# Slot experts: the last two experts' first matrices are loaded ahead of their second ones, and the tokens' keys and values are projected in pieces, with changes to routing and to the order of two engines

## The reference: what is computed

```
    o = q + _mha(q, x, x, d_...)                      # 16 slots of each batch
    h = layernorm(o)
    u = silu(h @ e_W1[e] + e_b1); g = silu(h @ e_Wg[e] + e_bg)
    o = o + (u * g) @ e_W2[e] + e_b2                  # slot e by expert e
    out = _mha(x, o, o, c_...)                        # keys o @ c_Wk, values o @ c_Wv
```

## Time and profile before

| what | before |
|---|---|
| median of 3 runs | 933.26 us (930.7 to 937.52) |
| profiled execution, own time | 932.76 us |
| its span in the trace | 931.0 us |
| PE busy | 827.4 us, 89% |
| DVE, ACT busy | 578.5 us, 511.6 us |
| routing block, until PE starts the next | 61.38 us |
| routed experts' last output product starts | 318.3 us |
| slot experts, first product to last result | 778.7 to 869.7 us |
| last block | from 871.0 us |

### The profile page before, as it was taken

The page is one execution under the profiler, slowest core; times in us unless marked ns, Lnnn a source line. Parts: engine busy times, 40 slices in busy tenths (PEclk is TensorE's granted clock), DMA queues, the critical chain, the costliest instruction groups (busy, mean ns, idle before and its releaser), DMA issues. The chain is left out here.

```text
span 931.0 us, 20572 instructions
## 1 busy us (share of the span) xinstructions
PE 827.4 (89%) x8132; PEld 705.6 (76%) x8132; DVE 578.5 (62%) x929; ACT 511.6 (55%) x935; POOL 196.0 (21%) x243
## 2 busy tenths in 40 slices
PE   5489999999999878999999989999998965976797
PEld 5389898999899756777788879999997952432354
DVE  3747778777787357887778855454435744321296
ACT  3138788788787245676767873433324432422364
POOL 0022434345343212234212222000000000000052
PEclk9599999999999989999999999999998986988799
DMA  7048676777684213432031112000008743998321
GB/s 294 1 174 324 209 286 214 271 260 253 214 301 131 62 52 81 87 74 42 19 137 48 41 52 92 1 1 1 1 1 341 295 197 118 425 427 348 125 82 69
DMA packets 70423, 143.21 MB, mean 154 GB/s; under 512 B 42504, under 2 KB 48136, under 8 KB 62904
## 3 DMA queue, kind: packets, MB, share of 16 engines
q1 hardware_dynamic: 64224, 127.25, 38.3%
q0 software_dynamic: 4496, 12.53, 3.9%
q10 hardware_dynamic: 1608, 2.12, 0.6%
HBM read 128.38 MB, written 13.50 MB: 152 GB/s over the span
## 5 line engine op out<-in xcount | busy, mean ns | idle before, releaser
L541 POOL DMA_INDIRECT results_of_experts<-k_w_ff,moew_place_of x39 | 56.1, 1439 | 147.4 <-DMA results_of_experts<-k_w_ff,moew_place_of 74.5
L87 PE MATMUL moe_pH<-moe_hh,moew_wh 128*128 128x256 f32 x256 | 72.5, 283 | 3.9 <-DVE moe_hl L758 3.9
L88 PE MATMUL moe_pH<-moe_hh,moew_wl 128*128 128x256 f32 x256 | 71.7, 280 | 0.0
L89 PE MATMUL moe_pH<-moe_hl,moew_wh 128*128 128x256 f32 x256 | 71.7, 280 | 0.0
L758 DVE TENSOR_TENSOR moe_hl<-k_w_ff,moe_hh 128x512 fp32r<-128x512 f32 x64 | 44.3, 691 | 33.9 <-ACT moe_hh L697 30.5
L688 ACT ACTIVATE k_w_ff<-moe_pH,moe_b 128x256 f32<-128x256 f32 x128 | 53.3, 467 | 17.8 <-PE moe_pH L89 13.4
L738 DVE TENSOR_TENSOR moew_wl<-k_x,moew_wh 128x1024 fp32r<-128x1024 f32 x45 | 53.4, 1218 | 1.3 <-ACT moew_wh L660 1.3
L738 DVE TENSOR_TENSOR moew_wl<-moew_raw,moew_wh 128x1024 fp32r<-128x1024 f32 x44 | 52.1, 1220 | 2.4 <-ACT moew_wh L660 2.2
L1710 DVE TENSOR_TENSOR k_w_ff<-attn_pS,k_w_ff 128x512 f32<-128x512 f32 x32 | 22.1, 691 | 50.3 <-PE attn_pS L89 34.6
L87 PEld LDWEIGHTS moe_pH<-moe_hh,moew_wh 128*128 128x128 f32 x256 | 48.2, 188 | 5.3 <-DVE moe_hl L758 5.3
L1484 ACT ACTIVATE attn_wh<-k_w_ff 128x512 fp32r<-128x512 f32 x32 | 20.2, 632 | 52.5 <-DVE k_w_ff L1710 52.5
(11 more groups left out here) (422 smaller groups left out, 2756.2 us busy)
## 6 DMA issues: line engine op xcount, KB each, us to landing
ring<-in_w_slot SPq DMA_DIRECT2D x10, 2048.0 KB
k_x<-in_w SPq DMA_DIRECT2D x24, 512.0 KB
k_x<-in_w SPq DMA_DIRECT2D x12, 1024.0 KB
moew_raw<-in_w SPq DMA_DIRECT2D x22, 512.0 KB
moew_raw<-in_w SPq DMA_DIRECT2D x11, 1024.0 KB
ring<-in_w_slot SPq DMA_DIRECT2D x9, 1024.0 KB, 16.8
k_w_ff<-in_w_slot SPq DMA_DIRECT2D x4, 2048.0 KB
attn_gat<-results_of_experts SPq DMA_DIRECT2D x16, 256.0 KB, 3.5
```

What stands on the lines that cost most here:

```text
L87: nc.tensor.matmul(out, ah, bh, start=start, stop=False)
L88: nc.tensor.matmul(out, al, bh, start=False, stop=False)
L89: return nc.tensor.matmul(out, ah, bl, start=False, stop=stop)
L541: nc.gpsimd.indirect_dma_start(out=dr.ys, out_offset=bass.IndirectOffsetOnAxis(ap=g.place_of[:, q:q + 1], axis=0), in_=ys[j % 2][:, s, :], ...
```

## The change

In routing: 9 and 18 unread matmuls in place of 28 and 40; the first tile's biases are loaded in this block, ahead of its matrices; ACT and DVE split matrix 0 and the first half of matrix 1 only, and the other 2048 columns at the start of the next block. In the routed experts: SP loads tiles 1's and 2's biases ahead of their matrices, and DVE does `weight_low(j, 2)` after both `hidden_low(j, 0, ...)` in a tile after a half tile. In the slot experts: `HALF_LENT` becomes 4; the stream ends with up 12, up 13, down 12, down 13; `pY` and `pR` exist once, and the banks saved hold keys and values, which are projected in five pieces of slots, as `PIECES` says (at the start of expert n's turn, and the last piece behind all experts); the last expert's `turn` comes ahead of the `down` of the one before; queries 0 and 1 are loaded at the stream's end into `w_small`. The last block starts with keys and values in place (also in `w_small`) and loads x1 first.

```diff
 # route
+            load_biases(sp, dr, w, 0, e)
+            load_matrices(sp, dr, w, 0, e)
...
-            for l in range(3):
+            for l in range(2):
                 act.wait_ge(w.raw_in[0][l], 16)
-                for c in range(2 if l == 1 else 1):
...
+                nc.scalar.activation(w.hi[0][l][:, 0:1024], w.raw[0][l][:, 0:1024], ACT.Copy).then_inc(w.hi_ok[l], 1)
...
-            for n in range(28):
+            for n in range(9):
...
-            for n in range(40):
+            for n in range(18):
...
 # routed_experts, SP, ACT, DVE
+            sp.wait_ge(x_in[0], moved(1, 0))
+            for j in range(1, NT):
+                e = sp.value_load(g.tile_expert[0:1, UNIT[j]:UNIT[j] + 1], min_val=0, max_val=E1 - 1)
+                if j < 3:
+                    load_biases(sp, dr, w, j, e)
+                load_matrices(sp, dr, w, j, e)
...
             x_high(0)
+            weight_high(0, 1, 1)
+            weight_high(0, 2)
...
             x_low(0)
+            weight_low(0, 1, 1)
             weight_low(0, 2)
...
                         hidden_low(j, 0, 0)
-                        weight_low(j, 2)
...
                     hidden_low(j, 0, 1)
+                    if j - 1 in HALVES:
+                        weight_low(j, 2)
...
-LENT, HALF_LENT = NS - 2, NS - 3
+LENT, HALF_LENT = NS - 2, 4
...
+PIECES = {7: (0, 4), 8: (NS - 2, NS), 11: (4, 8), NS - 1: (8, 12), NS: (12, NS - 2)}
...
 # slot_experts, SP
+            for e in STREAMED[:-2]:
+                up(e)
                 if e != HALF_LENT:
+                    down(e)
+            for e in STREAMED[-2:]:
+                up(e)
+            for e in STREAMED[-2:]:
+                down(e)
+            for i in range(2):
+                sp.dma_start(token_queries(g, i), dr.q[i:i + 1].rearrange("o p k n -> p (o k) n")).then_inc(q_in, 16)
+            sp.wait_ge(q_in, 16 * 2)
...
 # slot_experts, PE
+            def projected(n):
+                e0, e1 = PIECES[n]
+                p = list(PIECES).index(n)
+                pe.wait_ge(o_ok, max(ORDER.index(e) for e in range(e0, e1)) + 1)
+                for w, bank, done in ((W_CK, pK, k_sb), (W_CV, pV, v_sb)):
+                    if p > 0:
+                        pe.wait_ge(done, KD * p)
+                    for m in range(KD):
+                        for k in range(KD):
+                            last = nc.tensor.matmul(bank[:, m, 0:NB * (e1 - e0)], g.w_small[:, w, k, m * P:(m + 1) * P],
+                                                    g.o2T[:, k, e0:e1, :].rearrange("p e b -> p (e b)"), start=k == 0, stop=k == KD - 1)
+                    last.then_inc(kv_ps, 1)
+
             for n in range(NS):
+                if n in PIECES:
+                    projected(n)
                 up(n)
+                if n == NS - 1:
+                    turn(n)
                 if n > 0:
                     down(n - 1)
-                turn(n)
+                if n < NS - 1:
+                    turn(n)
                 if n > 0:
                     total(n - 1)
             down(NS - 1)
             total(NS - 1)
+            projected(NS)
...
 # tokens
-            slot_features(0, W_CK)
-            slot_features(1, W_CV)
             scores(0)
```

More of the change, by code:

```diff
@@ L460, in expert_weights @@
     w.x_in = [sem(f"xr_in{a}") for a in range(2)]
+    w.b12 = [sb(f"b12{a}", [P, 2 * KM]) for a in range(3)]
+    w.b3 = [sb(f"b3{a}", [P, D]) for a in range(3)]
+    w.b_in = [sem(f"b_in{a}") for a in range(3)]
     w.raw_in = [[sem(f"raw_in{l}{a}") for l in range(3)] for a in range(2)]
@@ L477, in routed_experts @@
         raw_in, wh_ok, wl_ok = w.raw_in, w.hi_ok, w.lo_ok
-        b12 = [sb(f"b12{a}", [P, 2 * KM]) for a in range(3)]
-        b3 = [sb(f"b3{a}", [P, D]) for a in range(3)]
+        b12, b3, b_in = w.b12, w.b3, w.b_in
         xh = sb("xh", [P, KD, SLOT], F32R)
@@ L494, in routed_experts @@
         x_in = w.x_in
-        b_in = [sem(f"b_in{a}") for a in range(3)]
         y_out = [sem(f"y_out{a}") for a in range(2)]
@@ L2279, in slot_experts @@
         pT = [ps(f"pT{a}", [P, 4, 4, NB]) for a in range(2)]
-        pY = [ps(f"pY{a}", [P, 512]) for a in range(2)]
-        pR = [ps(f"pR{a}", [P, 512]) for a in range(2)]
+        pY = ps("pY", [P, 512])
+        pR = ps("pR", [P, 512])
+        pK = ps("pK", [P, KD, PB])
+        pV = ps("pV", [P, KD, PB])
+        kv_ps, k_sb, v_sb = sem("kv_ps"), sem("k_sb"), sem("v_sb")
+        q_in = sem("q_in")
         hs_ok, a_ps, uc_ok, t_ps, ub_ok, us_ok, uf_ok, y_ps, yc_ok, r_ps, o_ok = (
@@ L2371, in sums, with keys @@
                     act.wait_ge(r_ps, n - 1)
-                nc.scalar.activation(yc[n % 2][:, :], pY[n % 2][:, 0:D], ACT.Copy).then_inc(yc_ok, 1)
+                nc.scalar.activation(yc[n % 2][:, :], pY[:, 0:D], ACT.Copy).then_inc(yc_ok, 1)
+            def keys(n):
+                e0, e1 = PIECES[n]
+                act.wait_ge(kv_ps, 2 * list(PIECES).index(n) + 1)
+                for m in range(KD):
+                    nc.scalar.activation(slot_features(g)[0][:, m, :, e0:e1].rearrange("p b e -> p e b"), pK[:, m, 0:NB * (e1 - e0)].rearrange("p (e b) -> p e b", b=NB),
+                                         ACT.Identity, bias=g.cols[:, COL_CBK, m:m + 1]).then_inc(k_sb, 1)
             for n in range(NS):
                 a = n % 2
+                if n in PIECES:
+                    keys(n)
                 act.wait_ge(a_ps, n + 1)
@@ L2384, in _ @@
             sums(NS - 1)
+            keys(NS)
         @block.vector
@@ L2388, in _, with values @@
             v = nc.vector
+            def values(n):
+                e0, e1 = PIECES[n]
+                dve.wait_ge(kv_ps, 2 * list(PIECES).index(n) + 2)
+                for m in range(KD):
+                    v.tensor_scalar(slot_features(g)[1][:, m, :, e0:e1].rearrange("p b e -> p e b"), pV[:, m, 0:NB * (e1 - e0)].rearrange("p (e b) -> p e b", b=NB),
+                                    g.cols[:, COL_CBV, m:m + 1], None, ALU.add).then_inc(v_sb, 1)
             def stationary(n):
@@ L2402, in _ @@
                 a = n % 2
+                if n in PIECES:
+                    values(n)
                 if n + 1 < NS:
@@ L2415, in _ @@
             result(NS - 1)
+            values(NS)
 def tokens(nc, g, dr):
@@ L2493, in _ @@
         def _(pe):
-            def slot_features(n, w):
-                for m in range(KD):
-                    for k in range(KD):
-                        last = nc.tensor.matmul(pVo[2 * n + m][:, :, :].rearrange("p k n -> p (k n)"), g.w_small[:, w, k, m * P:(m + 1) * P],
-                                                g.o2T[:, k, :, :].rearrange("p e b -> p (e b)"), start=k == 0, stop=k == KD - 1)
-                    last.then_inc(kv_ps, 1)
             def scores(i):
-                pe.wait_ge(q_in[i % 2], 16 * (i // 2 + 1))
+                if i >= 2:
+                    pe.wait_ge(q_in[i % 2], 16 * (i // 2))
                 pe.wait_ge(kx_ok, KD * (i + 1))
@@ L2567, in _ @@
         def _(act):
-            def slot_features(n, col, to):
-                for m in range(KD):
-                    act.wait_ge(kv_ps, KD * n + m + 1)
-                    nc.scalar.activation(to[:, m, :, :].rearrange("p b e -> p e b"), pVo[2 * n + m][:, :, :].rearrange("p k n -> p (k n)").rearrange("p (e b) -> p e b", e=NS),
-                                         ACT.Identity, bias=g.cols[:, col, m:m + 1]).then_inc(kv_sb, 1)
             def weights(i):
```

87 lines of the change are left out of this document (35 added, 52 removed).

## The result

| | before | changed |
|---|---|---|
| median | 933.67 us (4 runs, 930.7 to 937.52) | 921.88 us (4 runs, 920.87 to 925.71) |
| ratio | | 0.9887, 95% interval 0.9855 to 0.9918 |
| profiled execution: own time, span | 932.76, 931.0 us | 921.89, 920.1 us |

A forecast was written before the change was run, and what follows sets the result against it. PE, busy 89% of the span, was taken as the bound, with the weight stream at the slot experts' end. Gains 4.5 + 0.3 + 2.3 + 2.0 + 9.7 = 18.8 us gave 914.0 profiled, median 914.5 us, range 911 to 918.5.

The forecast's parts named there:

- Slot experts and last block (2.0 + 9.7 forecast): Last block starts 2.0 us earlier behind the slot experts; 9.7 us more since its projections no longer stand ahead.
- Up 12: Slot experts' weight stream: expert 12's up matrix was forecast to arrive at 848.2.
- The 0.9 us at the stream's start: Slot experts: up 5 issued earlier, behind expert 1's up product, was taken to gain 0.9 us (0 to 1.5).
- the low clock at 13%: Rival at the slot experts' end: the tail runs at the lower clock, 4.7 us less gain, 919 us; 13%.
- Half tiles (2.3 forecast): Routed experts: after a half tile, `hidden_low` comes 0.39 us earlier in six tiles, 2.3 us in all.
- The head (4.5 + 0.3 forecast): Routing: the second block's first product comes 4.5 us earlier; 0.3 us more from biases there early.
- The row products: Routing: with nine unread matmuls ahead, they end at 49.9 instead of 51.41, 1.5 us earlier.
- that rival: Routing: the head stays at the lower clock, products end at 50.8, head brings 1.3 us, 917.7 us; 8%.
- The two bias loads: Routing, on SP ahead of the matrices: 0.9 us of issues and 132 KB make the second matrix 1.2 us later.
- an estimated 3.9 us for the head: Routing: the head's 4.5 us gain, less about 0.6 us for the 4 KB load of `b12`.
- The slower one: Rival: PE's clock does not rise in the slot experts, PE becomes the bound, about 955 us; 3%.
- the wait for a load in the last block: Rival: x1 or queries are waited for as long as the projections took, 924 us; 2%.

The follow-up runs named there:

- biases_behind: The full change, with the first three tiles' biases loaded behind their tile's matrices instead of ahead: 921.42 us (4 runs), ratio 0.9871 to the kernel before.
- gather_first: The full change, with SP issuing tile 1's matrices only when tile 1's gathered rows have landed: 922.53 us (4 runs), ratio 0.9865 to the kernel before.
- slots_only: The kernel before with only the slot experts' and last block's part of the change: 925.35 us (10 runs), ratio 0.9901.
- before_warm50: The kernel before with 50 unread matmuls instead of 80 at the attention's start: 933.43 us (12 runs), ratio 0.9989.
- clock_kept: The full change with two unread matmuls behind each of the first three groups of row products: 925.84 us (one run).

## Why the forecast was wrong, point by point

- **Slot experts and last block (2.0 + 9.7 forecast): right in the sum, in part by luck.** 11.3 us in the trace. By parts: the last result 4.4 us earlier against the stage's start, as worked out (865.3 forecast, 865.82 its end, in a stage that began 0.5 us late). The steps inside it erred against each other. Up 12 arrived at 850.96 and not 848.2, which is 1.1 us earlier than before against the stage's start, and not 3.4. The 0.9 us at the stream's start did not come: from 780 to 810 us it moved 10.4 MB, before 10.6. And though 1 MB less stood ahead of up 12, as much had moved when its product started (27.9 MB by 851, 28.1 by 851.5 before); why later loads had come that far by then was not tested. PE then ran at full clock (1.92 us, 2.94 assumed), and the piece ended 1.1 us later than in my sum. The first reduction comes 2.2 us into the block (1.8 forecast). Over all traces with this part and its pieces unchanged, S + L runs from 91.9 to 94.6 against 103.9, by the clock at the last piece: a term of 9.3 to 12 us, where I put the low clock at 13% and for all pieces at once.
- **Half tiles (2.3 forecast): right, 2.1.** Each of the six waits fell from 0.59 to 0.24 us, 3.6 to 1.5 in all. M shows only 1.2 us because a gather is waited for 1.2 us at 230.7, where before one at 123.2 cost 0.7.
- **The head (4.5 + 0.3 forecast): wrong.** Three terms failed. The row products ended no earlier (1.5 forecast), since the clock was back at 0.50 for their second half, as in every trace with nine unread matmuls ahead of them; that rival had 8%, and its first half came true. This cost the head nothing yet, since DVE ended last, at 57.79, and PE's unread rows at 57.03; in biases_behind it did. What makes the clock fall there, the pause ahead of the products or the shorter row of matmuls before it, stays open. The two bias loads cost the first matrix 3.2 us, where I had 1.2 for the second, from issues and bytes: ACT's second piece came at 55.47 and not 53.7, and DVE's subtraction behind it 1.9 us late, which is all that the 4.5 us lack. The Trainium skill's page "DMA: Bandwidth & Descriptors", section on bandwidth, by whose figure for small transfers I had an estimated 3.9 us for the head instead of 4.5, pointed the right way; the trace has 2.6. Third, and largest, what came behind: H1 gained 2.6 us and H2 lost 2.7. I had priced what SP issues and in which order, but not *when* against the gather: the matrices ran beside the gather before too, but 2.4 us into the block, and now start at 1.8, with the rows there 9.5 us instead of 7.7 behind the block's start. gather_first shows that they delay it (5.2 us without them), and shows as well that the stretch has little slack to give: whichever transfer comes first, the other one is waited for. Why 0.6 us of earlier start costs 1.9 us is not shown.
- **The attention's start: missing.** No term of mine stood there, since the change touches nothing in it, and it took 1.6 us (A), with PE's first transposes 3.1 us later. All ten traces with the routing part and 80 unread matmuls have A at 461.4 us or more; of three without it, two have 459.6 and 459.9 and one 461.7. So the late rise is not the routing part's alone: slots_only and before_warm50, with the head of before, have 0.50 until 327 or 328 as well. What decides when the clock rises stays open. What the traces show is the price: where it rose late, 80 unread matmuls put PE's first transposes 3.4 to 6.2 us behind DVE, and 50 put them 2.1 to 2.5.
- **The rivals.** None of mine came true as a whole. The slower one and the wait for a load in the last block did not occur: the granted clock in the window 820 to 840 was 1.00, and from the first reduction to the end the last block took 44.62 us, as before (44.67).

## What to carry to other kernels

A transfer or wait that is taken off a queue lets everything behind it start earlier: ask what these will then run beside, and price the later of the two, not the one that moved. Work that exists only to hold a clock is critical whenever the clock is low, so count it at its slow price and make it end, at that price, where the real work becomes ready. A gain won upstream must be followed through each later point where PE meets something that did not move with it.

## What the runs showed of the hardware

- The granted clock stayed at 0.50 (1.2 GHz) for 11 us with PE busy without a gap (316 to 327 in the changed kernel), and for 10 us with hardly one (49 to 59 in clock_kept). At the first of these places, in the kernel before, 0.50 lasted from about 316.5 to 319.8.
- A float32 matmul of a 128 x 128 stationary with 64 columns costs as much as one with 128 at the full clock: 8 rows in 1.06 to 1.10 us against 1.06 to 1.16. At half the clock 8 rows with 192 columns took 2.77 to 2.93 us and with 64 columns 1.92 to 1.94.
- Two loads, one of 4 KB and one a broadcast of 1 KB to 128 partitions, moved 90 GB/s at a DMA share of 0.32 for 2 us and held the 0.5 MB load behind them up by 3.2 us, 1.05 of them in SP's issues.
